# Three one-column clears on GpSimd ahead of every gather of a recommendation tower

## The reference

```python
e = jnp.stack([tbl_0[ids[:, 0]], tbl_1[ids[:, 1]], ..., tbl_25[ids[:, 25]]], axis=1)   # (2048, 26, 128)
sd = jnp.einsum('bfd,bd->bf', sparse_values, dense_features)
ss = jnp.einsum('bfd,bgd->bfg', sparse_values, sparse_values)
pairs = ss[:, iu, ju]                      # iu, ju = triu_indices(26, k=1)
z = jnp.concatenate([dense_features, sd, pairs], axis=1)
h = jnp.concatenate([z, r_dense_features], axis=1)
h = jnp.maximum(h @ W_top1 + b_top1, 0.0)  # 607 -> 512
h = jnp.maximum(h @ W_top2 + b_top2, 0.0)  # 512 -> 256
y = h @ W_top3                             # 256 -> 1
```

## Time and profile before

| | us |
|---|---|
| median of 3 runs | 369.51 (367.83 to 371.0) |
| span of the profiled execution | 576.9 |
| TensorE busy in it | 398.2 (69%) |
| GpSimd busy in it | 255.3 (44%) |
| VectorE busy in it | 233.2 (40%) |
| ScalarE busy in it | 188.3 (33%) |
| mean granted TensorE clock in it | 0.805 |

### The profile page before, as it was taken

How to read it: one execution, slowest core, us unless ns; L and a number is a source line. 1 busy time by engine, 2 the same in 40 slices (tenths; PEclk the granted TensorE clock), 3 DMA queues, 4 the chain that set the end, 5 groups by cost and what they waited for, 6 DMA issues and landing times.

```text
span 576.9 us, 13714 instructions
## 1 busy us (share of the span) xinstructions
PE 398.2 (69%) x6224; PEld 348.2 (60%) x6224; DVE 233.2 (40%) x324; ACT 188.3 (33%) x283; POOL 255.3 (44%) x273
## 2 busy tenths in 40 slices
PE   5520875574948659496784938778495775969987
PEld 4410874462937649294673927758294664948876
DVE  6201877261522517343161631536333261543211
ACT  1110853241332324242142331334232332333553
POOL 6774826364262723626264261735516364361000
PEclk9865878595988859787696876979588795977999
DMA  8733105111010101101011010111102111110000
GB/s 216 196 91 76 42 22 185 26 42 38 24 47 20 50 25 34 50 17 42 25 47 43 19 43 17 55 30 33 47 7 59 25 43 34 28 42 16 2 2 3
DMA packets 11756, 26.84 MB, mean 47 GB/s; under 512 B 4653, under 2 KB 5805, under 8 KB 11571
## 3 DMA queue, kind: packets, MB, share of 16 engines
q0 software_dynamic: 8512, 17.45, 11.6%
q1 hardware_dynamic: 3186, 8.52, 5.3%
HBM read 25.95 MB, written 0.01 MB: 45 GB/s over the span
## 4 chain that ended last, share of the span: by engine, by line
PE 55%; another core or an unknown queue 20%; issue 14%; ACT 9%; DVE 0%; DVEq 0%
PE sum_bank L589 21%; PE vec_bank L616 10%; PE work L650 7%; PE work L641 6%; ACT vecT L423 4%; PE vec_bank L602 4%; PE work L637 3%; ACT vecT L415 3%; PE id_bank L563 1%; ACT late L439 1%; PE work L630 1%; PE work L726 1%; ACT parts L392 0%; PE work L656 0%
## 5 line engine op out<-in xcount | busy, mean ns | idle before, releaser
L308 POOL DMA_INDIRECT rows<-in_tbl,ids_all x266 | 254.4, 957 | 265.2 <-PE vec_bank L602 152.0
L343 DVE TENSOR_TENSOR onehot<-id_bank,row_f 125x1024 fp32r<-125x1024 f32 x150 | 176.8, 1217 | 285.7 <-remote 114.5
L589 PE MATMUL sum_bank<-onehot,parts 125*128 125x256 f32 x1152 | 179.4, 300 | 50.4 <-issue 32.6
L589 PEld LDWEIGHTS sum_bank<-onehot,parts 125*128 125x128 f32 x1152 | 159.3, 199 | 56.7 <-issue 49.5
L616 PE MATMUL vec_bank<-vecT 128*26 128x26 f32 x4096 | 60.2, 204 | 74.1 <-issue 42.8
L616 PEld LDWEIGHTS vec_bank<-vecT 128*26 128x26 f32 x4096 | 50.8, 117 | 90.7 <-issue 61.9
L423 ACT COPY vecT<-vec_bank 128x512 f32<-128x512 f32 (+1 forms) x74 | 83.2, 1128 | 66.9 <-remote 30.0
L415 ACT COPY vecT<-sum_bank 128x256 f32<-128x256 f32 x75 | 52.3, 697 | 106.7 <-remote 59.0
L641 PE MATMUL work<-late,w_all 126*128 126x256 f32 (+1 forms) x192 | 59.5, 455 | 20.0 <-issue 18.3
L641 PEld LDWEIGHTS work<-late,w_all 126*128 126x128 f32 x192 | 43.2, 237 | 31.2 <-issue 21.6
L650 PE MATMUL work<-late,w_all 128*128 128x256 f32 x112 | 41.8, 540 | 20.0 <-ACT late L439 13.9
(11 more groups left out here) (40 smaller groups left out, 107.1 us busy)
## 6 DMA issues: line engine op xcount, KB each, us to landing
rows<-in_tbl,ids_all POOLq DMA_INDIRECT x266
late<-in_tbl SPq DMA_DIRECT2D x7, 480.0 KB
w_all<-in_weights SPq DMA_DIRECT2D x1, 1571.0 KB
w_all<-in_tbl SPq DMA_DIRECT2D x3, 480.0 KB
xT<-in_dense_t SPq DMA_DIRECT2D x8, 128.0 KB
vecT<-in_ids_t SPq DMA_DIRECT2D x1, 256.0 KB, 2.9
late<-in_weights SPq DMA_DIRECT2D x1, 256.0 KB
ids_all<-in_ids SPq DMA_DIRECT2D x1, 208.0 KB, 2.5
```

Source lines behind the costliest of these rows:

```text
L308: nc.gpsimd.indirect_dma_start(rows[:, tile % TD, FG * j + n, :], None, tables[f], bass.IndirectOffsetOnAxis(ids_all[:, tile, f:f + 1], 0) ...
L343: nc.vector.tensor_tensor(onehot[:, use % RING, 0:width, :], bass.AP(got.tensor, got.offset, [got.ap[0], [0, width], [1, DS]]), bass.AP(nu ...
L589: last = nc.tensor.matmul(into_sum, parts[:, k, CH_AT[n] + c0 + c, :], hot, start=first and k == 0, stop=final and k == PARTS - 1)
```

## The change

A tile `spacer` of 128 partitions, 3 x 272 floats, is added. Ahead of every gather GpSimd clears three columns of it, of one float per partition each, with three instructions. No two of them write the same column, and nothing reads the tile. No semaphore is added, and no other engine's program changes.

```diff
 LATE_SPLIT = 4
+SPACERS = 3
@@
+        spacer = sb("spacer", [P, SPACERS, TILES * NG])
         ids_all = sb("ids_all", [P, TILES, FEATS], i32)
@@
                     if tile >= TD:
                         pool.wait_ge(vec_filled, rows_at(same_rows(tile, j)[-1], j) + 1)
                     for n, f in enumerate(group(j)):
+                        for k in range(SPACERS):
+                            nc.gpsimd.memset(spacer[:, k, tile * NG + FG * j + n:tile * NG + FG * j + n + 1], 0.0)
                         nc.gpsimd.indirect_dma_start(
                             rows[:, tile % TD, FG * j + n, :], None, tables[f],
                             bass.IndirectOffsetOnAxis(ids_all[:, tile, f:f + 1], 0)
```

## The result

| | before | after |
|---|---|---|
| median of 10 runs each, us | 368.99 | 371.97 |
| ratio (95% interval) | | 1.0067 (1.0045 to 1.0088) |
| span of the profiled execution, us | 576.9 | 370.4 |
| GpSimd busy, share of the span | 255.3 (44%) | 302.8 (82%) |
| TensorE busy, share of the span | 398.2 (69%) | 343.2 (93%) |

The kernel became slower by 0.7%: 2.5 us by the ratio (1.7 to 3.2), 3.0 us by the medians. I had forecast 397 us and at least 374: the direction is right, the added time is about a ninth of the 27.5 us I had forecast. By my own line of 1% between a difference and none, this is "same", to which I had given 0.10. The span of the recorded execution is of no use for the difference: that of before was stretched (the first experiment records it again). Apart from it one run fell far out, 532.36 us with twelve clears, at a mean granted clock of 0.565.

What follows compares the result with a forecast made beforehand. GpSimd's chain of gathers was taken as the bound: a floor of 359.4 us, plus 34.6 for the clears (266 x 0.13), plus 3 of waits left in place, gives 397 us; range 374 to 430.

Steps and rivals of the forecast that it cites:

- What bounds the kernel: Whole kernel: GpSimd's chain of gathers holds 97% of the time, with TensorE loaded almost alike.
- The floor by GpSimd: GpSimd's chain without waits: 3.5 to first gather, 333.9 gathers and gaps, 1.2 landing, 20.8 last tile; 359.4 us.
- TensorE's 332 us: TensorE's matmuls and transposes, priced from unbroken stretches, sum to 332 us without any wait between engines.
- Case 4: GpSimd isn't the bound: it gathers faster unprofiled, or TensorE's work and waits make 369.5; 370 to 376 us, chance 0.06.
- The pace of a clear: Back-to-back 128x1 clears on GpSimd: steps of 0.037 us, so three cost 0.11 us if the engine only keeps pace.
- I expect it not to be done beside clears either: The 0.30 us ahead of a gather is its own preparation; three clears add 0.13 us per gather, 34.6 us in all.
- this second case: Not slower: the clears run inside the 0.30 us ahead of a gather; 369.5 us, chance 0.09.
- The slack: GpSimd waits of at most 10.1 us, at the start and in steps 3, 5 and 7; 3 us left in place.
- The signs I named: Next profile: gather spacing 1.38, 1.25 or at least 1.55 us tells cases apart; gather stays 0.94, span within 10 of 576.9.
- my case: GpSimd's chain takes each three clears at 0.09 to 0.23 us; 383 to 425 us, chance 0.74.

Runs made afterwards that it cites:

- the first experiment: The kernel before, recorded once more with no edit (also called the second recording of before); its span is 368.1 us.
- the light kernel: Kernel before with 576 of the 1152 lookup matmuls left out and no clears: 365.66 us, ratio 0.9906, span 363.9 us.
- run 6: Not a label, but part of "made the run 6% slower": six clears ahead of every gather, against the kernel before; 390.83 us, ratio 1.061.

## Why the prediction was wrong

**What bounds the kernel: right in the main.** The stretched recording was seen as such; the spacing of 1.25 us, taken as the one rhythm that recording had not broken, is that of the unstretched one. The floor by GpSimd, 359.4, was too low: the span of the light kernel puts it at 363.9. The terms that were short are the gathers' time (254.4 us against 257.4), their gaps (79.5 against 82.9 less the first wait of 2.1) and the landing (2.1 us after the start against 2.7). TensorE's 332 us stood too low as well: its busy time is 342.8. Case 4 (GpSimd is not the bound, 0.06) fits only in part: TensorE's bound is 1.4 us below the time of the kernel before, and no gathering faster than recorded was needed for that. I had GpSimd as the longer of the two by 27 us (359.4 against 332); the runs put TensorE's bound (367.2) even a little above GpSimd's (365.7).

**The pace of a clear: nearly right.** I read 0.037 us from the ends of four rows; it is 0.028. The starts of the same rows, 0.03 apart, were the better reading.

**The step that failed: "I expect it not to be done beside clears either".** From a gather starting 0.28 us behind its releaser I concluded that the 0.30 us between two gathers is preparation that nothing else can share. The rows behind it were right, the conclusion was not. Of the 0.305, only 0.15 must lie behind the end of what stands ahead; the other 0.15 is room. Three clears need 0.17. The term came out at 0.017 us per gather instead of 0.13, and 4.5 us instead of 34.6. My argument against that case, that the gap is never filled by a gather's own work, said nothing on what short instructions could do in it; only a row with another instruction in the gap could have, and the trace of before has none behind a gather. I gave this second case 0.09. It came true only up to its edge: one clear ahead of each gather moved no gather at all, three cost 4.5 us of chain, and six made the run 6% slower.

**The slack: wrong place, about the right size.** I put up to 10.1 us of waits at the start and in steps 3, 5 and 7, and let 7 of them be used up. There were no such waits on GpSimd; what absorbs is that TensorE is up to 4 us late against the gathers, and this change lost 1.5 of its 4.5 us there. With the measured price, my sum with 3 us kept gives 359.4 + 4.5 + 3 = 366.9, which is less than the kernel before takes; with all of the 10.1 kept it gives 374.0, 2.0 above the measured time. So even with the right price the floor and the slack term would have been off by as much as the effect.

**The two rules of the Trainium skill.** "Perfetto Trace Analysis", GPSIMD Engine Instruction: timing by start-to-start spacing was the right advice here, at 28 ns for each further clear against recorded durations of 113. Identifying the Most-Contended Engine judges GpSimd by its occupancy and TensorE by the busy share of its weight loads. In the unstretched recording that is 70% against 85%, so it names TensorE, yet taking 48 us of busy time from TensorE gains 3.0 us. Occupancy misses a chain whose gaps of 0.30 us don't count as busy.

**The signs I named.** 1.38 us of spacing for my case, 1.25 for the second: 1.266 says the second, nearly. The gather's duration stayed at 0.94. The span "within about 10 us of 576.9" failed with the stretched execution on which it was built.

## What to carry to other kernels

The idle time in front of an instruction, where the profile names no one who was waited for, isn't all taken: a part of it can hold short work of the same engine. Find out with one, three and six cheap instructions rather than reasoning it out; the curve has a flat piece and then a slope, and a change can sit on either. And spread such work over the gaps: the same 798 clears cost 3 us in threes and 13 in twelves.

Where two engines are close, take work from each in turn. Here the two runs gained 1.4 and 3.0 us, and that bounds the slack directly; the waits of the first recording, 190 us on GpSimd, would have misled.

## What the runs showed of the hardware

- Between two gathers on GpSimd lie 0.305 us. Clears begin at the end of the gather before and the next gather starts 0.15 us behind their end (0.16 behind a wider one), or at 0.305 if that is later: gaps of 0.305, 0.322, 0.407 and 0.577 for 1, 3, 6 and 12 clears.
- A clear of one column costs 28 ns in a row of clears although its recorded duration is 113 to 118 ns; one of 64 columns was recorded at 166, one of 128 at 220.
- Six gathers near the start take 1.85 us instead of 0.94. In the second recording of before, GpSimd and VectorE there:

```profile
19.58 1.84 POOL L308 DMA_INDIRECT rows<-in_tbl,ids_all  x1 [0.30 <-issue]
...
22.98 1.85 POOL L308 DMA_INDIRECT rows<-in_tbl,ids_all  x1 [0.30 <-issue]
```
```profile
19.40 1.22 DVE L322 TENSOR_TENSOR parts<-late,parts 125x1024 fp32r<-125x1024 f32 x1
20.53 2.35 DVE L343 TENSOR_TENSOR onehot<-id_bank,row_f 125x1024 fp32r<-125x1024 f32 x2
22.79 1.22 DVE L322 TENSOR_TENSOR parts<-late,parts 125x1024 fp32r<-125x1024 f32 x1
```

  Each long gather starts inside a subtraction of VectorE whose two inputs are both in SBUF (L322) and ends about 0.8 us behind that one's end; beside the compares (L343, one input in PSUM) gathers keep their 0.94. With six and twelve clears gathers happen to start at other points of the same subtraction, 0.28 to 0.85 us into it; they take 1.77 to 1.19 us and still end 0.81 to 0.82 us behind its end. One that starts within the first 0.04 us of it keeps its 0.94 to 0.95. The Trainium skill, "SBUF — State Buffer", Who interferes with whom, says that a VectorE instruction with two SBUF inputs contends with a GpSimd instruction that reads SBUF; the rows agree, as a gather reads its ids there. The same section reports of a probe that such a `tensor_tensor` did not stall DMA; the rows here speak against that for gathers. These six cost about 5.4 us of GpSimd's chain (6 x 0.91). No run took the subtractions away to try it.
